# Moving the step sizes of three scan directions off VectorE: a 16x16 image network on one core

## The reference, cut to what matters

```python
def step(h, inp):
    dt, bt, ct, ut = inp
    h = jnp.exp(dt[..., None] * A) * h + (dt * ut)[..., None] * bt[:, None, :]
    return (h, jnp.einsum('bdn,bn->bd', h, ct))
...
dts = jnp.einsum('kbrl,kdr->kbdl', dt_stack, dt_w)
delta = jax.nn.softplus(dts + dt_b[:, None, :, None])
A = -jnp.exp(A_logs)
ys = jax.vmap(_selective_scan)(xs, delta, A, Bst, Cst, Ds)
y = ys.sum(0)
...
# attention: 8 heads, 7 x 7 neighbours
attn = attn + jnp.transpose(bias, (0, 1, 3, 2, 4))[None]
attn = jax.nn.softmax(attn.reshape(b, nh, h, w, k * k), axis=-1)
```

## Time and profile before

| what | value |
|---|---|
| median of 3 runs | 324.97 us (323.05 to 325.08) |
| the profiled execution: its own time | 318.75 us |
| the profiled execution: span on the core | 317.0 us |
| mean granted TensorE clock | 0.965 of full speed |

### The profile page before, as it was taken

The page is one execution under the profiler, slowest core; times in us unless marked ns, Lnnn a source line. Parts: engine busy times, 40 slices in busy tenths (PEclk is TensorE's granted clock), DMA queues, the critical chain, the costliest instruction groups (busy, mean ns, idle before and its releaser), DMA issues.

```text
span 317.0 us, 4939 instructions
## 1 busy us (share of the span) xinstructions
PE 265.6 (84%) x1711; PEld 133.1 (42%) x1721; DVE 249.8 (79%) x655; ACT 152.6 (48%) x340; POOL 126.7 (40%) x96
## 2 busy tenths in 40 slices
PE   6976298767877697898899988999999997999982
PEld 3322022212221122332455566776556654656541
DVE  3229999999999999999687687646758648798956
ACT  2058056534453335336076648848581366544331
POOL 4002366689868989888140024440000100002102
PEclk9799789999999799789999999999999999999998
DMA  6990000000000000000500000000000000000000
GB/s 191 333 404 39 0 3 0 1 2 0 0 0 3 0 0 0 2 0 1 200 1 2 0 1 3 2 0 3 0 2 0 3 1 0 2 1 2 0 10 8
DMA packets 5290, 9.68 MB, mean 31 GB/s; under 512 B 2721, under 2 KB 3425, under 8 KB 5010
## 3 DMA queue, kind: packets, MB, share of 16 engines
q1 hardware_dynamic: 5266, 9.37, 8.4%
HBM read 9.24 MB, written 0.13 MB: 30 GB/s over the span
## 4 chain that ended last, share of the span: by engine, by line
PE 42%; DVE 37%; issue 8%; ACT 7%; POOL 5%; DMA 1%; POOLq 0%; DVEq 0%; ACTq 0%
DVE arena L1464 12%; PE ps L969 6%; PE ps L954 6%; DVE arena L1454 5%; PE ps L840 5%; PE ps L762 3%; DVE x L1596 2%; PE ps L1126 2%; DVE arena L1822 2%; PE ps L984 2%; PE ps L1113 2%; PE ps L866 2%; PE ps L729 2%; DVE arena L1596 2%; PE ps L1190 2%
## 5 line engine op out<-in xcount | busy, mean ns | idle before, releaser
L468 POOL TENSOR_TENSOR arena<-arena 128x1024 f32<-128x1024 f32 x31 | 76.3, 2460 | 26.0 <-DVE arena L1464 22.0
L1464 DVE TENSOR_TENSOR_SCAN arena<-ps,arena 128x1024 f32<-128x1024 f32 x32 | 72.8, 2278 | 0.1
L550 ACT ACTIVATE ps<-ps,aneg 128x510 f32<-128x510 f32 x64 | 39.5, 655 | 63.8 <-PE ps L840 63.8
L840 PE MATMUL ps<-arena 32*128 32x510 f32 x128 | 39.3, 699 | 25.1 <-DVE arena L1454 20.8
L433 POOL TENSOR_TENSOR rstd<-ve,mhalf 128x2 f32<-128x2 f32 (+1 forms) x14 | 10.4, 742 | 100.3 <-DVE ve L1335 93.5
L846 PE MATMUL ps<-arena 32*128 32x512 f32 x128 | 39.4, 699 | 0.7 <-DVE arena L1454 0.7
L1454 DVE TENSOR_TENSOR arena<-ps,arena 128x1024 f32<-128x1024 f32 x32 | 38.7, 1210 | 0.7 <-PE ps L846 0.4
L599 ACT ACTIVATE arena<-ps,cols 128x256 f32<-128x256 f32 x64 | 25.4, 472 | 13.6 <-PE ps L956 12.9
L840 PEld LDWEIGHTS ps<-arena 32*128 32x128 f32 x128 | 10.6, 199 | 40.2 <-DVE arena L1454 24.9
L1596 DVE SCALAR_TENSOR_TENSOR x<-ps,ww,x 128x64 f32<-128x64 f32 x86 | 18.0, 276 | 7.4 <-PE ps L984 7.3
L884 PE MATMUL ps<-idle 128*128 128x512 bf16 x78 | 20.7, 380 | 1.1 <-issue 0.6
(11 more groups left out here) (221 smaller groups left out, 538.7 us busy)
## 6 DMA issues: line engine op xcount, KB each, us to landing
arena<-in_w SPq DMA_DIRECT2D x5, 512.0 KB, 6.4
bias<-in_rpb SPq DMA_DIRECT2D x1, 1408.0 KB, 8.4
w<-in_w SPq DMA_DIRECT2D x2, 512.0 KB, 6.1
arena<-in_w SPq DMA_DIRECT2D x1, 1024.0 KB, 10.8
arena<-in_w_conv SPq DMA_DIRECT2D x1, 576.0 KB, 3.8
c<-in_c SPq DMA_DIRECT2D x1, 512.0 KB, 4.4
w_bc<-in_w_bc SPq DMA_DIRECT2D x1, 512.0 KB, 5.7
arena<-in_spread SPq DMA_DIRECT2D x1, 256.0 KB, 5.8
```

The source lines that it names most:

```text
L468: pool.tensor_tensor(hc[:, i % HC_SLOTS], states[i % 4], c_all, ALU.mult).then_inc(hc_done, 1)
L550: act.activation(a, a, ACT.Exp, scale=aneg[:, q:q + 1]).then_inc(exp_done, 1)
L840: pe.matmul(dst, spread[rows_, m], src, start=True, stop=True).then_inc(dspread, 1)
L1464: dve.tensor_tensor_scan(h, decay_banks(i).rearrange("p s l -> p (s l)"), h, 0.0, ALU.mult, ALU.add).then_inc(scan_done, 1)
```

## The change

- Directions 1 to 3: `small_log`, `delta_log` and `delta` leave VectorE. GpSimd gets products and sums of two tables (`small_log`, `summed`, `delta`); the constants that VectorE's three-operand instructions added move to ScalarE (an Identity activation with a column behind the log and behind the square, the square scaled by the root of the leading coefficient).
- Directions 2 and 3: `bounded_from`, `bounded_to` and `bounded_one` leave VectorE. ScalarE makes relu(z - 2^-6) (`ranged`) and the two additions (`ones_of`); GpSimd makes zmin as a difference (`rest_of`). Direction 1 keeps VectorE's, ahead of the loop.
- `delta_u(1)` moves from VectorE (pair 4) to GpSimd (pair 2).
- VectorE's loop holds `times_b(i + 1)` and scan i for every pair, product 1 ahead of scan 0.
- TensorE: reversed and mixed inputs stand ahead of the loop of pairs; matmuls by zeros are also issued in pairs 1 and 2. ScalarE copies the reversed input in pair 1.
- The mask is in the bias table that is loaded; `mask_head` and the window table (2 x 176 columns of the constants) are gone.

```diff
-BOUNDED_AT = {5: 2, 13: 3}
-LOST_AT = {8: 2, 16: 3}
-LOG_AT = {0: 1, 8: 2, 16: 3}
-LOG1P_AT = {9: 2, 17: 3}
-SMALL_LOG_AT = {0: 1, 9: 2, 17: 3}
-DELTA_LOG_AT = {1: 1, 10: 2, 18: 3}
-DELTA_AT = {2: 1, 11: 2, 19: 3}
-DELTA_U_AT = {12: 2, 20: 3}
-MASK_AT = [9, 10, 16, 17, 18] + list(range(20, 31))
+RANGED_AT = {5: 2, 13: 3}
+REST_AT = {5: 2, 13: 3}
+ONES_AT = {6: 2, 14: 3}
+LOST_AT = {7: 2, 15: 3}
+LOG_AT = {7: 2, 15: 3}
+SQUARE_AT = {8: 2, 16: 3}
+LOG1P_AT = {8: 2, 16: 3}
+SMALL_AT = {9: 2, 17: 3}
+SUMMED_AT = {10: 2, 18: 3}
+DELTA_AT = {0: 1, 11: 2, 19: 3}
+DELTA_U_AT = {2: 1, 12: 2, 20: 3}
...
# GpSimd
+            def rest_of(k):
+                pool.wait_ge(z_ready, k + 1)
+                pool.wait_ge(over_ready, k - 1)
+                pool.tensor_tensor(zmin[k], z_[k], zmax[:, k], ALU.subtract).then_inc(rest_ready, 1)
+            def small_log(k):
+                pool.wait_ge(square_ready, k + 1)
+                pool.tensor_tensor(z_[k], z_[k], zmin[k], ALU.mult).then_inc(small_ready, 1)
+            def summed(k):
+                pool.wait_ge(relu_ready, k + 1)
+                pool.wait_ge(log1p_ready[1], k)
+                pool.tensor_tensor(z1[k], z1[k], dd[:, k, 0], ALU.add).then_inc(summed_ready, 1)
+            def delta(k):
+                pool.wait_ge(small_ready, k)
+                pool.wait_ge(summed_ready, k)
+                pool.tensor_tensor(dd[:, k, 0], z_[k], z1[k], ALU.add).then_inc(delta_ready[1], 1)
             lost(pool, 1)
             log1p(pool, 1)
+            summed(1)
+            small_log(1)
...
                 pool.tensor_tensor(hc[:, i % HC_SLOTS], states[i % 4], c_all, ALU.mult).then_inc(hc_done, 1)
+                if i in REST_AT:
+                    rest_of(REST_AT[i])
                 if i in LOST_AT:
...
-                if i in MASK_AT:
-                    mask_head(MASK_AT.index(i))
# ScalarE
+            def ranged(k):
+                act.wait_ge(bounds_set, 5)
+                act.wait_ge(z_ready, k + 1)
+                act.activation(zmax[:, k], z_[k], ACT.Relu, bias=minus_from[:]).then_inc(over_ready, 1)
+            def ones_of(k):
+                act.wait_ge(over_ready, k - 1)
+                act.activation(z1[k], zmax[:, k], ACT.Identity, bias=one_from[:]).then_inc(plus_ready, 1)
+                act.wait_ge(plus_ready, k - 1)
+                act.activation(z1[k], z1[k], ACT.Identity, bias=minus_one_from[:]).then_inc(back_ready, 1)
...
+                act.wait_ge(log_raw, k)
+                act.wait_ge(minus_log_ready, 1)
+                act.activation(dd[:, k, 1], dd[:, k, 1], ACT.Identity, bias=minus_log_at[:]).then_inc(log_ready, 1)
...
+                act.activation(z_[k], zmin[k], ACT.Square, bias=root_c1[:], scale=ROOT_C2).then_inc(square_raw, 1)
+                act.wait_ge(square_raw, k)
+                act.activation(z_[k], z_[k], ACT.Identity, bias=root_c0[:]).then_inc(square_ready, 1)
...
                 decays(i)
-                if i == 2:
+                if i == 0:
+                    log_of(1)
+                    square(1)
+                if i == 1:
                     act.wait_ge(rev_ps, 1)
                     act.activation(u[:, 1], bank(7), ACT.Copy).then_inc(u_back_ready, 1)
# TensorE
             got("c16", "c32")
+            reversed_input()
+            mixed_input()
             for i in range(1, PAIRS):
...
-                if i == 1:
-                    reversed_input()
-                if i == 2:
-                    mixed_input()
...
-                elif 2 < i < PAIRS - 2:
+                elif i < PAIRS - 2:
                     add_zeros(2 if makes_bc or i in DTS_AT else 3 if i % 2 else 6)
# VectorE
-                if 0 < i < PAIRS - 1:
+                if i + 1 < PAIRS:
                     times_b(i + 1)
...
-                if i == 0:
-                    times_b(1)
-                if i in BOUNDED_AT:
-                    bounded_from(BOUNDED_AT[i])
...
-                if i in DELTA_AT:
-                    delta(DELTA_AT[i])
-                if i == 4:
-                    delta_u(dve, 1)
...
-            dve.wait_ge(bias_ready, 2 * HEADS)
+            dve.wait_ge(load["rpb"], 16)
# tables
+        o["rpb"][:, q] = np.where(in_window(q)[:, None], o["rpb"][:, q], -BIG)
```

More of the change, by code:

```diff
@@ L355, in delta_u, with delta_made @@
                 eng.wait_ge(u_ready, 1)
-                eng.wait_ge(u_back_ready, 2)
-            eng.wait_ge(delta_ready, k + 1)
+            if k % 2:
+                eng.wait_ge(u_back_ready, k // 2 + 1)
+            eng.wait_ge(*delta_made(k))
             eng.tensor_tensor(dd[:, k, 1], dd[:, k, 0], u[:, k], ALU.mult).then_inc(u_made(k)[0], 1)
+        def delta_made(k):
+            return delta_ready[k > 0], max(k, 1)
         def u_made(k):
-            return delta_u_ready[k // 2], k % 2 + 1
+            return delta_u_ready[k > 0], max(k, 1)
         def lost(eng, k):
-            eng.wait_ge(z1_ready, k + 1)
+            if k < 2:
+                eng.wait_ge(z1_ready, k + 1)
+            else:
+                eng.wait_ge(back_ready, k - 1)
             eng.tensor_tensor(z1[k], zmax[:, k], z1[k], ALU.subtract).then_inc(lost_ready[k > 0], 1)
@@ L444, in _ @@
             pool.tensor_tensor(rstd[:, 0], ve[:, 0], mhalf[:, 0], ALU.pow).then_inc(rstd_ready, 1)
+            for column, value in ((minus_from, -LOG_FROM), (one_from, 1.0 + LOG_FROM), (minus_one_from, -1.0 - LOG_FROM),
+                                  (root_c1, ROOT_C2 * LOG_C1 / 2), (root_c0, LOG_C2 * (LOG_C0 - LOG_C1 ** 2 / 4))):
+                pool.memset(column[:], value).then_inc(bounds_set, 1)
             pool.memset(w_i2[:], 0.0).then_inc(w_i2_padded, 1)
[L447 to L453, removed]
+            def rest_of(k):
[13 more added lines that the diff above has]
+                pool.tensor_tensor(dd[:, k, 0], z_[k], z1[k], ALU.add).then_inc(delta_ready[1], 1)
             lost(pool, 1)
             log1p(pool, 1)
+            summed(1)
+            small_log(1)
             for i in range(PAIRS - HC_ON_DVE):
@@ new lines, in ones_of @@
+            def ones_of(k):
[3 more added lines that the diff above has]
+                act.activation(z1[k], z1[k], ACT.Identity, bias=minus_one_from[:]).then_inc(back_ready, 1)
+            def log_of(k):
+                if k == 0:
+                    act.wait_ge(zmax_ready, 1)
+                    act.activation(dd[:, k, 1], zmax[:, k], ACT.Ln, bias=1.0).then_inc(log_ready, 1)
+                    return
+                if k == 1:
+                    act.wait_ge(zmax_ready, 2)
+                    act.activation(dd[:, k, 1], zmax[:, k], ACT.Ln, bias=1.0).then_inc(log_raw, 1)
+                else:
+                    act.wait_ge(over_ready, k - 1)
+                    act.activation(dd[:, k, 1], zmax[:, k], ACT.Ln, bias=one_from[:]).then_inc(log_raw, 1)
+                act.wait_ge(log_raw, k)
+                act.wait_ge(minus_log_ready, 1)
+                act.activation(dd[:, k, 1], dd[:, k, 1], ACT.Identity, bias=minus_log_at[:]).then_inc(log_ready, 1)
@@ new lines, in square @@
+            def square(k):
+                if k == 0:
+                    act.wait_ge(zmin_ready, 1)
+                    act.activation(z_[k], zmin[k], ACT.Square, bias=half_c1[:]).then_inc(square_ready, 1)
+                    return
+                act.wait_ge(bounds_set, 5)
+                if k == 1:
+                    act.wait_ge(zmin_ready, 2)
+                else:
+                    act.wait_ge(rest_ready, k - 1)
+                act.activation(z_[k], zmin[k], ACT.Square, bias=root_c1[:], scale=ROOT_C2).then_inc(square_raw, 1)
+                act.wait_ge(square_raw, k)
+                act.activation(z_[k], z_[k], ACT.Identity, bias=root_c0[:]).then_inc(square_ready, 1)
@@ L576, in _ @@
                 decays(i)
-                if i == 2:
+                if i == 0:
+                    log_of(1)
+                    square(1)
+                if i == 1:
                     act.wait_ge(rev_ps, 1)
                     act.activation(u[:, 1], bank(7), ACT.Copy).then_inc(u_back_ready, 1)
+                if i in RANGED_AT:
+                    ranged(RANGED_AT[i])
+                if i in ONES_AT:
+                    ones_of(ONES_AT[i])
                 if i in LOG_AT:
                     log_of(LOG_AT[i])
-                    square(LOG_AT[i])
+                if i in SQUARE_AT:
+                    square(SQUARE_AT[i])
                 if i in PREPARED_AT:
@@ L1909 @@
 C32_AT, C32_COLS = _places([("anti", P), ("state_sum", PER_GROUP * 32),
[L1910 removed]
+                            ("tap_sum", 5 * CH), ("rank8", TB * 8), ("rank16", TB * 16)])
 C16_AT, C16_COLS = _places([("tri", P), ("ones", P)])
@@ L1944, in constants @@
         c["tap_sum"][i[ok], r * CH + rows[r][ok] // TAPS] = 1
[L1945 to L1952, removed]
     c["rank8"][:] = np.tile(8 - np.arange(8), TB)
@@ L1958, in constants, with in_window @@
```

(6 more changed lines are left out.)

60 lines of the change are left out of this document (30 added, 30 removed).

## The result

| | before | after |
|---|---|---|
| median | 324.01 us (319.5 to 325.08, 4 runs) | 310.43 us (308.76 to 311.44, 4 runs) |
| profiled execution, its span | 318.75, 317.0 | 309.88, 308.0 |
| first product to end of last scan | 119.57 | 109.12 |
| scan 0 to scan 25, start to start | 96.34 | 83.18 |
| scan 25 to scan 30 | 17.51 | 19.20 |

The ratio is 0.9677 (95% interval 0.962 to 0.9733).

The account below looks back on a forecast made before the run. VectorE's own instruction stream was taken to bound the loop. 12.5 - 0.3 - 0.2 = 12.0 us off 318.75 gives 306.75; with 6.2 carried over to the runs' median, 313.0 us, range 310.5 to 318.

Parts of the forecast that it names:

- The surplus: VectorE's loop, scan 0 to 25: 96.34 us against 82.75 at the bare pace; 12.5 to win after 1.11 for order.
- The other sum: Cross-check over VectorE's 16 removed instructions: 12.5 busy, less 1.3 overlap, plus 0.5 waiting for GpSimd, giving 11.7 us.
- The mask ... lie beside other work: 0: GpSimd's 16 mask instructions, 8.8 us in the window: nothing the loop waits for stands behind them, so removal gains 0.
- The order: Product 1 (1.11 us) moved ahead of scan 0: said to cost VectorE nothing.
- 0.7 to 0.8 late costs 0 to 0.1: delta_u(3) on GpSimd, ending at 55.0 and wanted by TensorE at 54.33: lateness mostly absorbed, costing 0 to 0.1 us.
- the 0.3 charged for both directions: Allowance of 0.3 us for step sizes of directions 2 and 3 coming late from GpSimd.
- The rival of GpSimd's pace: GpSimd sets the pace of pairs 5 to 20; gain 6 to 9 us, taken as 317 us; chance 0.09.
- its pair with a bc copy and the log's two: Among ScalarE's fullest pairs: decays 1.15, the two 1.35, copy 0.6, together 3.1 of the 3.31 us pace.
- The pair of prepared(2): ScalarE's longest pair, decays 3.95 us apart: 0.64 late against 0.78 of room, a margin of 0.14, costing nothing.
- the charge of 0.2: Allowance of 0.2 us for TensorE's reversed and mixed inputs ahead of pair 2's spreads running at the lower clock.
- Pairs 26 to 30, where the bias blocks run, are left as they are: End of the loop, left unchanged; stalls beside the bias blocks could go as well, another microsecond.
- the ring of states: Four states let GpSimd's hc lag 4.2 us before VectorE waits; hc 21 counted 2.05 late, so no stop.

Follow-up runs that it names:

- e8: Changed kernel with four zero matmuls behind the bias blocks of pairs 24 and 26, and delta_u(3) ahead of hc of pair 20: median 305.54 us, ratio 0.9492.
- e7: Changed kernel with the zero matmuls, plus one unused sum of two SBUF tables on VectorE behind each scan of pairs 6 to 13: 314.41 us, ratio 0.9764.
- e3: Kernel before with only the mask put into the loaded bias table: median 322.46 us, ratio 1.0045.
- e4: Kernel before with only the order changed (product 1 ahead of scan 0, reversed and mixed inputs ahead of the pairs, zeros from pair 1): 320.50 us, ratio 0.9972.
- e1: The changed kernel run once more, with no edit: median 311.04 us, ratio to before 0.9591.
- e10: The changed kernel run again, unedited, on one chip with two other runs: median 309.02 us, ratio to before 0.9578.
- e2: Changed kernel with four matmuls by zeros behind the bias blocks of pairs 24 and 26: median 307.61 us, ratio to before 0.9593.
- e5: Changed kernel with the zero matmuls, but directions 2 and 3 done as in the kernel before (step sizes on VectorE): 312.31 us, ratio 0.9717.

## Why the prediction was right

*The surplus.* 12.5 was read from the distance of the scans, and 12.51 is what e8 shows for the loop free of it. The other sum, 11.7, was low because it took an overlap off every instruction: pair 9's step in the kernel before is 1.13 over the pace with the 1.06 of L1413 in it. That VectorE's instructions are worth about their length is e7's result too, 0.73 for each 0.67.

*Mask and order.* "The mask ... lie beside other work: 0" was wrong as an attribution: it cost 1.06 (e3). Half is the wait of direction 3, where a mask instruction (100.12, 1.00 long) delayed the GpSimd result that L1421 reads, so something that the loop waited for did stand behind it; half is the longer L1421. The sum had already counted both with VectorE's lines. The order costs nothing, as put, but also made L1413 1.3 shorter (e4). The total stands, but part of what was put down to VectorE's lines was the mask's and the order's.

*GpSimd.* hc runs at 2.355 in the mean. hc 21 was counted to begin 2.05 late; it begins at 107.18, 2.2 behind the end of scan 21 (104.96, where the next product starts). delta_u(3) ends at 107.21, 55.3 behind the end of scan 5 (51.96), where 55.0 was counted.
```profile
105.95 1.26 POOL L366 TENSOR_TENSOR arena<-arena 128x512 f32<-128x512 f32 x1
107.18 4.67 POOL L503 TENSOR_TENSOR arena<-arena 128x1024 f32<-128x1024 f32 x2
```
"0.7 to 0.8 late costs 0 to 0.1" was low: 0.38, against the 0.3 charged for both directions (direction 2 cost nothing). The product begins 0.25 late, and the scan 1.24 behind it instead of 1.11: VectorE, having waited, lost the overlap of the two as well, which the count had left out. The rival of GpSimd's pace didn't come: no product waited for hc.

*ScalarE and TensorE's start.* No step from pair 1 to 22 is over 3.32, so ScalarE hides all it was given; its pair with a bc copy and the log's two leaves nothing between the decays at 54.62 and those at 57.70, 3.08 apart where 3.1 was counted. The pair of prepared(2) takes 3.94, and its decays end at 49.62, 0.15 ahead of scan 5; the margin was put at 0.14. The reversed and mixed inputs ran at the higher clock, 1.10 and 1.88; the charge of 0.2 was not needed.
```profile
33.44 1.10 PE L884 MATMUL ps<-arena,c 128*128 128x512 f32 x2
34.37 1.88 PE L879 MATMUL ps<-arena,d_mix 128*128 128x512 f32 x4
```

*What came by luck.* "Pairs 26 to 30, where the bias blocks run, are left as they are": they are not alike from one execution to the next, 17.5 to 21.2 us without zeros in either loop, and the prediction allowed a microsecond for it. The start, 28.2 to 32.0, moves as much. The profile of before was a quick one in both, and the changed kernel's lost 1.69 more beside the bias blocks, so that VectorE's loop took 109.12 there where about 107 was forecast. The gain is 8.9 by the two profiles and 13.6 by the medians. The same two kernels gave the ratios 0.9677, 0.9591 (e1) and 0.9578 (e10). The forecast's 12.0 is right by its mechanism for the loop up to scan 25, where 12.14 was measured; that the whole time came as close is in part luck, since each of the two moving stretches can shift a run by nearly 4 us, a third of the gain.

## What to carry to other kernels

Where one engine never waits, the distance of its repeated instruction's starts, less the same distance in a stretch that holds nothing else, gives what may be won, and it was right to a tenth here; the sum over lines was 0.8 low. When work moves to an engine with spare time, count the lag pair by pair and compare it with every consumer's deadline; the one that was missed here was the first use of the next direction and not the ring of states. Before comparing two profiles' totals, compare a stretch that the edit doesn't touch.

## What the runs showed of the hardware

The spreads beside the bias blocks, matmuls of one column, ran at the lower clock level in all six executions without zeros, and shortly in two of the seven with them (e2, e8). More surprising was the first 8 us: the same eight matmuls ahead of the loop (16x128) took 1.15 us in four of the thirteen executions, 1.33 and 1.48 in two and 2.04 to 2.07 in seven, with a granted clock of 1.00 recorded from 4.4 to 7.9 in executions of either kind (e5 and the changed kernel). In the seven the first product started at 30.93 to 31.71; in five of the other six it started at 28.20 to 29.80, and in e7, which has two more instructions on GpSimd ahead of the loop, at 31.96.
```profile
4.45 1.15 PE L825 MATMUL ps<-arena 16*128 16x128 f32 x8
```
```profile
4.45 2.07 PE L830 MATMUL ps<-arena 16*128 16x128 f32 x8
```
The first is e5's, the second the changed kernel's; TensorE has the same instructions up to there in both. What sets it wasn't found: kernels with either loop had the slow form, and the granted clock doesn't show it.
